# Test-time-trained attention with a SwiGLU FFN on one core: projection, x1 and FFN moved six slots forward against the scan, with z re-laid step by step

## The reference, cut to what matters

```
def step(W, kv):                       # 16 tokens of one head
    z = kc @ W
    grad = kc.T @ ((z - vc) * inv_n)
    return W - LR * grad, z
z = scan(step, eye, (rope(x @ Wk.T), x @ Wv.T))
x1 = norm(x + (norm(z) * gamma + beta) @ Wo.T)
out = norm(x1 + (silu(x1 @ gate.T * gs) * (x1 @ up.T * us)) @ down.T * ds)
```

## Time and profile before

| | us |
|---|---|
| median of 3 runs (2057.78 to 2060.44) | 2058.8 |
| the profiled execution's own time | 2054.83 |
| its span, first to last instruction | 2052.7 |
| TensorE busy | 1949.6 |
| VectorE busy | 1219.4 |
| ScalarE busy | 938.1 |
| GpSimd busy | 582.4 |

### The profile page before, as it was taken

The page is one execution under the profiler, slowest core; times in us unless marked ns, Lnnn a source line. Parts: engine busy times, 40 slices in busy tenths (PEclk is TensorE's granted clock), DMA queues, the critical chain, the costliest instruction groups (busy, mean ns, idle before and its releaser), DMA issues.

```text
span 2052.7 us, 54706 instructions
## 1 busy us (share of the span) xinstructions
PE 1949.6 (95%) x22424; PEld 1550.6 (76%) x22424; DVE 1219.4 (59%) x2814; ACT 938.1 (46%) x2258; POOL 582.4 (28%) x651
## 2 busy tenths in 40 slices
PE   5669999999999999999999999999999999998887
PEld 3347877778787777878777787877778787777775
DVE  3484665666566566656656665665666566565532
ACT  2324444444444444445444444544444454444421
POOL 2012323223332322333232233323323332332332
PEclk9769999999999999999999999999999999999999
DMA  6842222222332222232222223222222322222110
GB/s 208 265 132 82 86 88 60 82 73 86 94 88 86 61 82 71 87 95 85 89 60 83 67 90 94 87 87 59 85 73 84 94 88 86 63 82 56 49 35 21
DMA packets 211019, 176.61 MB, mean 86 GB/s; under 512 B 34193, under 2 KB 165521, under 8 KB 210577
## 3 DMA queue, kind: packets, MB, share of 16 engines
q1 hardware_dynamic: 210768, 173.08, 28.2%
HBM read 105.86 MB, written 75.76 MB: 88 GB/s over the span
## 4 chain that ended last, share of the span: by engine, by line
PE 90%; DVE 5%; ACT 2%; issue 1%; SPq 1%; DMA 1%; POOL 0%; POOLq 0%; DVEq 0%
PE gu_acc L616 35%; PE work L597 28%; PE down_acc L628 14%; PE state_acc L587 5%; PE z_acc L570 4%; PE work L604 3%; PE gu_acc L604 1%; DVE err L799 1%; DVE fm L828 1%; ACT fm L475 1%; SPq L286 1%; DVE low_half L864 1%; DVE hid L806 1%; ACT hid L451 1%; DMA v_rows<-v_scr 0%
## 5 line engine op out<-in xcount | busy, mean ns | idle before, releaser
L799 DVE TENSOR_TENSOR err<-z_acc,v_rows 32x256 f32<-32x256 f32 x1024 | 430.0, 420 | 177.8 <-PE z_acc L570 148.9
L378 POOL TENSOR_TENSOR hid_lo<-hid,hid_hi 128x256 fp32r<-128x256 f32 x352 | 267.2, 759 | 912.0 <-ACT hid_hi L461 911.9
L427 ACT ACTIVATE state<-state_acc 32x256 f32<-32x256 f32 x1028 | 385.5, 375 | 87.9 <-PE state_acc L587 63.9
L616 PE MATMUL gu_acc<-x_hi,gw 128*128 128x256 f32 x1408 | 385.8, 307 | 8.6 <-DVE x_lo L843 3.6
L616 PE MATMUL gu_acc<-x_hi,uw 128*128 128x256 f32 x1408 | 349.7, 281 | 0.0
L616 PE MATMUL gu_acc<-x_lo,gw 128*128 128x256 f32 x1408 | 349.6, 281 | 0.0
L616 PE MATMUL gu_acc<-x_lo,uw 128*128 128x256 f32 x1408 | 349.3, 281 | 0.0
L806 DVE SCALAR_TENSOR_TENSOR hid<-gu_acc,up_scale,hid 128x256 f32<-128x256 f32 x352 | 170.2, 484 | 297.3 <-ACT hid L451 296.4
L440 ACT ACTIVATE v_rows<-z_acc 128x256 f32<-128x256 f32 x256 | 98.6, 385 | 521.3 <-DVE err L799 521.3
L616 PEld LDWEIGHTS gu_acc<-x_hi,gw 128*128 128x128 f32 x1408 | 266.0, 189 | 59.8 <-DVE hid L806 23.8
L628 PE MATMUL down_acc<-dw,hid_hi 128*128 128x512 f32 x704 | 284.2, 404 | 2.8 <-POOL hid_lo L378 2.8
(11 more groups left out here) (67 smaller groups left out, 2117.3 us busy)
## 6 DMA issues: line engine op xcount, KB each, us to landing
x_fm<-xT SPq DMA_DIRECT2D x64, 256.0 KB, 3.3
k_scr<-k_tok SPq DMA_DIRECT2D x32, 512.0 KB, 2.9
k_rows<-k_scr SPq DMA_DIRECT2D x512, 32.0 KB, 1.9
v_rows<-v_scr SPq DMA_DIRECT2D x512, 32.0 KB, 1.8
z_scr<-v_rows SPq DMA_DIRECT2D x512, 32.0 KB, 1.7
z_tok<-z_scr SPq DMA_DIRECT2D x32, 512.0 KB, 3.9
x_tok<-x SPq DMA_DIRECT2D x32, 512.0 KB, 3.5
out<-x_tok SPq DMA_DIRECT2D x32, 512.0 KB, 2.9
```

The source lines that it names most:

```text
L378: pool.tensor_tensor(hid_lo[m % RING][:], hid[m % 2][:], hid_hi[m % RING][:].bitcast(F32), ALU.subtract).then_inc(hid_lo_ready, 1)
L427: act.activation(state[q, :, e].rearrange("p (r g) e -> p r g e", r=2), state_acc[q, :, 0:P].rearrange("p r (g e) -> p r g e", e=HEAD), AC ...
L616: mm = pe.matmul(gu_acc[:, k * TOK:(k + 1) * TOK], lhsT=w[:, c, m * P:(m + 1) * P].bitcast(dt), rhs=part[:, c].bitcast(dt), start=(c == 0 ...
L799: dve.tensor_tensor(err[q, g:g + 2, :, :].rearrange("p a (r h) e -> p a r (h e)", r=2), z_acc[q, :, 0:P].rearrange("p r (a c) -> p a r c", ...
```

## The change

The pipeline is cut again. Tile t is now projected within tick t (K of sequence 0 in slot 6, V in 7, K of sequence 1 in 8, V in 9 to 11, the turns of K in 12 and 13) and scanned in tick t+1. The tile scanned in the tick before has its z turned in slots 2 and 3, is projected by Wo in 4 and 5, and its x1 is turned in 8 and 9. Its FFN follows at once: `gate_up` 0 to 5 in slots 10 to 15 of the same tick (`EARLY_GU`), 6 to 10 in slots 0, 1, 2, 3 and 6 of the next (`LATE_GU`); the `down` blocks follow a slot behind, and the last layer norm is in slots 11 to 14. The ticks go from 0 to 34, 35 instead of 37.

z is stored in a layout of its own, [step, partition, 2, 128], in three transfers (steps 0 to 3, 4 to 6, 7), with both halves of each partition's row, and loaded with two 32 KB transfers per step. `k_scr` and `v_scr` are one tile deep; v's first half is loaded per sequence.

In the first two ticks: the split of V's weights comes in slot 5 of tick 0, ahead of the high part of x's second sequence on ScalarE; ScalarE issues the copies and the loads of the FFN's weights; the bias matmuls are in slot 14 of tick 0 and the split of Wo in its slot 15, ahead of the first `copy_state`; the twelve maxima are spread by `WEIGHED` over slot 3 of tick 1 to slot 5 of tick 2, and TensorE branches ahead of slot 10 of tick 2. The wait on `zeroed` before each scan half is gone. The counts are written with plain integers; `nk`, `nb`, `ncc`, `nd`, `ny` become `t`, `sc`, `o`, `f1` and `f2`, `y`.

The core of the diff (the new order of the ticks; the old one stands in the listing above):

```diff
-GU_SLOTS = (0, 1, 2, 3, 4, 5, 6, 7, 8, 11, 13)
-DOWN_SLOTS = (1, 2, 3, 4, 5, 6, 7, 8, 9, 13)
+FFN_SLOT = 10
+EARLY_GU, LATE_GU = {10: 0, 11: 1, 12: 2, 13: 3, 14: 4, 15: 5}, {0: 6, 1: 7, 2: 8, 3: 9, 6: 10}
+EARLY_DOWN, LATE_DOWN = {11: 0, 12: 1, 13: 2, 14: 3, 15: 4}, {0: 5, 1: 6, 2: 7, 4: 8, 7: 9, 9: 10}
+WEIGHED = {3: (0,), 5: (1,), 7: (2,), 9: (3,), 11: (4, 5), 13: (6, 7), 15: (8,), 17: (9,), 19: (10,), 21: (11,)}
...
-        k_scr = nc.dram_tensor("k_scr", [2, BATCH, P, DM], F32, kind="Internal").ap()
-        v_scr = nc.dram_tensor("v_scr", [2, BATCH, P, DM], F32, kind="Internal").ap()
-        z_scr = nc.dram_tensor("z_scr", [BATCH, SEQ, DM], F32, kind="Internal").ap()
+        k_scr = nc.dram_tensor("k_scr", [BATCH, P, DM], F32, kind="Internal").ap()
+        v_scr = nc.dram_tensor("v_scr", [BATCH, P, DM], F32, kind="Internal").ap()
+        z_scr = nc.dram_tensor("z_scr", [NS, P, 2, P], F32, kind="Internal").ap()
...
+            def store_z(n, i0, i1, stored):
+                if i0 == 0 and n >= 1:
+                    sp.wait_ge(zn_turned, 2 * n)
+                sp.wait_ge(z_saved, NS * n + i1)
+                sp.dma_start(z_scr[i0:i1].rearrange("i p q c -> p i q c"), v_rows[:, i0:i1]).then_inc(z_stored, 16)
+            def load_z(n, i0, i1, stored):
+                sp.wait_ge(z_stored, 48 * n + stored)
+                for i in range(i0, i1):
+                    for p in range(2):
+                        src = z_scr[i].rearrange("(h p t) q c -> p q t h c", p=2, t=MB)[p, p]
+                        dst = z_tok[i * MB:(i + 1) * MB].rearrange("t b (a p c) -> t (b a) p c", a=2, p=2)[:, :, p]
+                        sp.dma_start(dst, src).then_inc(z_tok_in, 16)
...
+                sc, o, y = t - 1, t - 2, t - 3
+                if within(sc) and sc >= 1:
+                    load_half1(sc)
+                if within(sc):
+                    store_z(sc, 0, NS // 2, 16)
+                    load_z(sc, 0, NS // 2, 16)
+                if within(t) and within(t + 1):
+                    load_x_fm(t + 1)
+                if within(t):
+                    store_v(t, 0)
+                    store_k(t)
+                    if t == 0:
+                        sp.wait_ge(state_begun, 2 * HQ)
+                    load_k_half0(t)
+                    store_v(t, 1)
+                if within(sc):
+                    store_z(sc, NS // 2, NS - 1, 32)
+                if within(t):
+                    load_v_half0(t, 0)
+                    load_v_half0(t, 1)
+                if within(sc):
+                    load_z(sc, NS // 2, NS - 1, 32)
+                    store_z(sc, NS - 1, NS, 48)
+                    load_z(sc, NS - 1, NS, 48)
+                if t == 0:
+                    load_half1(0)
+                if within(y):
+                    sp.wait_ge(y_ready, 2 * y + 2)
+                    sp.dma_start(out[:, rows(y), :].rearrange("b t f -> t b f"), y_tok[:]).then_inc(out_stored, 16)
+                if within(sc):
+                    load_x(sc)
...
+                    if within(t) and s == 6:
+                        high_x(t, 1)
+                    if within(t) and s == 8:
+                        copy_v(t, 0)
+                    if within(t) and s == 12:
+                        copy_v(t, 1)
+                    if within(o) and s == 8:
+                        high_x1(o, 0)
...
+                    if within(f2) and s in (2, 6):
+                        gate(f2, LATE_GU[s])
+                    if within(o) and s == 2:
+                        high_zn(o, 0)
+                    if within(sc):
                         if s % 2 == 0:
+                            save_z(sc, s // 2)
                         else:
+                            keep_state(sc, s // 2)
+                    if within(o) and s == 3:
+                        high_zn(o, 1)
...
+                    if t == 0 and s == 5:
                         act.wait_ge(wv_in, 16 * NC)
                         for c in range(NC):
                             high_part(wv, (x_tok, z_tok), c)
+                        for i in range(3):
+                            copy_ffn(i)
...
+                    if t == 0 and s == 15:
+                        for c in range(NC):
+                            act.wait_ge(wo_scaled, c + 1)
+                            high_part(wo, x1_tok, c)
+                        act.wait_ge(zeroed, 6)
+                        act.wait_ge(state_begun, 2 * HQ)
+                        copy_state()
+                        act.wait_ge(small_in, 16 * 7)
+                        load_ffn(0)
+                    if t == 1 and s in (3, 9):
+                        load_ffn((s + 3) // 6)
...
+            def tick(t, ffn_dt=None, first=0, last=SLOTS):
+                sc, o, f1, f2 = t - 1, t - 2, t - 2, t - 3
+                for s in range(first, last):
+                    if within(sc):
                         if s % 2 == 0:
+                            scan_z(sc, s // 2)
                         else:
+                            scan_state(sc, s // 2)
+                    if within(o) and s == 3:
+                        turn_z(o, 1)
+                    if within(o) and s in (8, 9):
+                        turn_x1(o, s - 8)
+                    if within(t) and s == 13:
                         turn_k(t, 1)
+                    if within(f2) and s in (7, 9):
+                        down(f2, LATE_DOWN[s], ffn_dt)
+                    if within(f2) and s in LATE_GU:
+                        gate_up(f2, LATE_GU[s], ffn_dt)
+                    if within(f1) and s in EARLY_GU:
+                        gate_up(f1, EARLY_GU[s], ffn_dt)
+                    if within(o) and s == 2:
+                        turn_z(o, 0)
+                    if within(o) and s in (4, 5):
+                        project_o(o, s - 4)
+                    if within(t) and s in (6, 8):
+                        project_k(t, (s - 6) // 2)
+                    if within(t) and s == 7:
+                        project_v(t, 0, 0, NC)
+                    if t == 0 and s == 9:
+                        begin_state()
+                    if within(t) and s in (9, 10, 11):
+                        project_v(t, 1, *((0, 2), (2, 3), (3, 4))[s - 9])
+                    if within(t) and s == 12:
                         turn_k(t, 0)
+                    if within(f2) and s in (0, 1, 2, 4):
+                        down(f2, LATE_DOWN[s], ffn_dt)
+                    if within(f1) and s in EARLY_DOWN:
+                        down(f1, EARLY_DOWN[s], ffn_dt)
+                    if t == 0 and s == 14:
+                        find_bias()
+            def rest(ffn_dt):
+                tick(2, ffn_dt, FFN_SLOT, SLOTS)
+                for t in range(3, NT + 3):
+                    tick(t, ffn_dt)
+            tick(0)
+            tick(1)
+            tick(2, None, 0, FFN_SLOT)
...
+                sc, o, f1, f2, y = t - 1, t - 2, t - 2, t - 3, t - 3
                 for s in range(SLOTS):
+                    if within(o) and s == 6:
+                        add_o(o, 1)
+                    if within(sc) and s % 2 == 0:
+                        scan_err(sc, s // 2)
+                    if within(o) and s == 3:
+                        low_zn(o, 1)
+                    if within(t) and s == 6:
+                        low_x(t, 1)
+                    if within(t) and s in (7, 9):
+                        rotate(t, (s - 7) // 2)
+                    if within(o) and s == 6:
+                        dve.wait_ge(o_added, 2 * o + 2)
+                        moments_of(1, o, x_tok)
+                    if within(t) and s == 13:
+                        copy_k_cols(t, 1)
+                    if within(y) and s == 11:
+                        scale_y(y)
+                    if within(y) and s == 13:
+                        dve.wait_ge(y_added, 2 * y + 2)
+                        moments_of(2, y, y_tok)
+                    if within(f2) and s in LATE_GU and s != 6:
+                        scale_hid(f2, LATE_GU[s])
+                    if within(f2) and s == 7:
+                        scale_hid(f2, 10)
+                    if within(f1) and s in EARLY_GU:
+                        scale_hid(f1, EARLY_GU[s])
+                    if within(o) and s == 0:
+                        dve.wait_ge(z_tok_in, 256 * (o + 1))
+                        moments_of(0, o, z_tok)
+                    if within(o) and s == 1:
+                        normalize(0, o, z_tok, z_tok, zn_ready)
+                    if within(o) and s == 2:
+                        low_zn(o, 0)
...
+                    if within(o) and s == 7:
+                        if o >= 2:
+                            dve.wait_ge(y_added, 2 * (o - 1))
+                            dve.wait_ge(x1_turned, 2 * (o - 1))
+                        normalize(1, o, x1_tok[o % 2], x_tok, x1_ready)
+                    if within(o) and s in (8, 9):
+                        low_x1(o, s - 8)
+                    if within(t) and s == 12:
```

(12 more changed lines are left out.)

683 lines of the change are left out of this document (266 added, 417 removed).

## The result

The changed kernel takes 2064.8 us (median of 8 runs, 2062.1 to 2067.3) where the kernel before takes 2058.8 (8 runs beside them, 2056.9 to 2060.4): a ratio of 1.0029, with a 95% interval of 1.0018 to 1.0040. It is slower by 6 us. The forecast was 2058, no change that can be measured.

A forecast was written before the change was run, and what follows sets the result against it. TensorE's own work, about 59.65 us a tick, was taken to bound the middle. Steady ticks +19, tick 31 +3, end -26 and start +3 gave -1 against the 2052.7 span; predicted median 2058 us, range 2038 to 2080.

The forecast's parts named there:

- the start's +3: Everything up to tick 3: tick 3 starts at 164 us instead of 161.1, +3 (-4 to +10).
- tick 1's 54: Tick 1: 41 for eight steps, 7 for projections, 2 to 4 for gate weights, 3 for weighings; tick 2 starts at 99.
- The first rival: Steady tick's waits stay hidden and the ends give; tick 3 starts at 158, whole 2042 us; chance 0.27.
- (a): Steady tick, first rotation, before V: only a scan half and one down cover 1.45 us; cost 0.2 us (0 to 0.4).
- (c): Steady tick, second turn of K: the copy of the first half's columns now stands behind scale_hid; cost 0.2 us (0 to 0.48).
- (d): Steady tick, first output projection: high part of z's second half comes behind the state copies; cost 0.15 us (0 to 0.4).
- (e): Steady tick, gate-up 0 to gate-up 1: 3.15 us of work between them against a 3.24 us loop; cost 0.1 us.
- (b): Steady tick, VectorE must be free when K ends: 5.0 us of queue against 5.45; margin about 0.36 us, cost 0.
- The close-up of the last gate-ups: At the end, last tile: gate-ups 9 and 10, before spaced by slots with waits, run closer; 2 us less.
- VectorE late to the first rotation: Rival, slot 7: VectorE 1 us late makes the tick pay 0.6 more, 17 us on top, 2075 us; chance 0.24.
- Waits hidden: Rival, steady tick: (a) to (e) cost 0.3 us together, +9 over the middle; whole 2042 us; chance 0.27.
- Late z: Rival, each tick: z's store and loads take 9 us instead of 5.2, moments_of waits about 1; some 2080 us; chance 0.06.

The follow-up runs named there:

- the run without cover: Changed kernel with down 9 of slot 7 moved behind the V projections, so nothing lies between scan and V: 2092.1 us, mean tick 61.29.
- the spread run: Changed kernel with only the gate copy in tick 0, gate load and two copies at 40 us, other loads after scan 1's first rows: 2057.7 us, ratio 0.9998.
- all three runs of the dose: Changed kernel with one, two or three FFN weight copies in tick 0 and the gate load behind scan 0's rows: 2059.4, 2052.0 and 2055.5 us.

## Why the prediction was wrong

**The step that failed** is the start's +3, and in it two terms. "Rows of scan 0 must share with the 8.6 MB of weight copies ... now the copies have ScalarE's queue. I take 45": the scan, whose start needs no rows of v, began at 40.98, before the 43 to 48 laid out; its first state half, which needs them, came at 65.3. The forecast had no term for the time between the two. And "2 to 4 for VectorE waiting for the gate weights" was the only price put on the loads. That 45 and tick 1's 54 should have given 99 for tick 2; it was 111.9. The working had the evidence in hand, the v store of 23.4 us behind the same copies, and set it aside because the copies had another queue. The runs showed that the queue gave no protection: the store took 24.2 us behind three copies on ScalarE's queue too. In the kernel before that delay fell where hardly anyone waited (VectorE 1.60 us), behind the last loads of scan 0's first rows in the same queue (the copies began at 37.7) and with scan 1's rows not needed until 98.8. The change moved K and V to the middle of the tick. From their stores to the scan that needs them there is now less than half a tick, and the z transfers stand in the same queue. Without the traffic tick 3 starts at 157, 7 us before the 164 laid out. The work itself was priced too long, and this hid a part of the miss. The first rival's 158 is near that number, but it was meant with the traffic.

**The steady tick** held in its terms: (a) 0.20 of 0.2, (c) 0.20 of 0.2, (d) 0.14 of 0.15, (e) 0.13 of 0.1, and the turn of z at 0.20 as before. The mean of ticks 4 to 30 grew from 59.84 to 60.35, by 0.51 and not by 0.67; the dropped waits on `zeroed` did not give the 0.16. Cut at the first matmul of each block and averaged over ticks 4 to 29, the scan halves of a tick grew by 0.44 us, the downs by 0.07 and the projections by 0.06, while the gate-ups fell by 0.05 and the turns by 0.01. With the four waits taken off, every kind of block is 0.01 to 0.05 shorter, and that is the 0.16: the kernel before had small waits beyond the 0.19 that the forecast took for the only one, and "In the middle a new order can only add waits" was not quite true. (b) was right at 0, though its rows leave a margin of 0.45 and not 0.36: V waits for the rotation itself and no longer than (a) has it. The +16.5 is 27 times 0.51, tick 31's 3.8 (forecast as 3) and 0.9 less in tick 3.

**The end** was forecast at -26 and came at -24.9. The close-up of the last gate-ups, -2, didn't come.

**Rivals.** VectorE late to the first rotation: no, though the run without cover shows its price, 27 us for 0.94 a tick. Waits hidden: no, all four show. Late z: not in the steady state, where the turn of z waits 0.20 as it did; the Trainium skill's rule on small transfers (DMA: Bandwidth & Descriptors, Rules for kernel authors) has no trace there. In tick 2 of the spread run it was z that paid, 15.45 us, but to weight loads and not to its own small pieces.

The same page of the Trainium skill, in its section on queues, rings and completion order, says that a DMA engine goes round its queues packet by packet and finishes a packet before it turns to the next. Two queues would then share one set of engines, which the forecast did not weigh when it took ScalarE's queue for a protection. The trace agrees with the sharing: 24.2 us behind three copies from another queue. It does not look like taking turns, by which one would expect 256 KB to be through long before 8.6 MB: the store landed about 2 us after the last copy in all three runs of the dose, as if it stood in line behind them. How much of that is the held issue of the last section, no run here shows.

## What to carry to other kernels

A transfer of megabytes is not free merely because its own result is needed late: price it by the small transfers of every queue that will be issued while it moves, and ask who waits for those. When work moves later relative to its consumer, check what bulk traffic its old slack was hiding, here in the first three ticks and not in the steady state; and when a wait goes from place to place with each new layout, run both kernels without the suspected traffic, which gives the two floors at once.

## What was not expected of the hardware

An issue on SyncE took 8.6 us with two copies under way on ScalarE's queue and 18.7 with three, against 0.34 with one: the issuing engine itself is held. So all that stands behind it in its program is late as well. It is not the number of copies alone: in the kernel before, with three copies ahead in SyncE's own queue, the store at 44.15 was issued in 0.35 us and still landed 23.4 us later, and it was the loads of v's rows at 57.33 that were held (9.65 us for eight). What decides how long an issue is held, no run shows.

The kernel before varies by a few us from execution to execution, and its profiled one was 4 us below its median. In the run of the old order without weights, the last 16.5 us of tick 31 have a mean granted clock of 0.74, a part of them at the lower of the levels 1.2 and 2.4 GHz, and TensorE busy for 11.4; tick 31 lasted 59.5 us. In the profiled execution of before, the same stretch:

```profile
1880.00:1894.70 14.70, 9.44 (x166) 7.12 (x165) 8.33 (x20) 7.93 (x21) 2.15 (x3) 1.00 0.04 8
```

Full clock, and the tick took 56.7. These 3 us would fit most of the distance between that profile and the median, and with it most of why the medians differ by 6.0 where the two profiles differ by 11; the changed kernel's tick 31 is full and has no such stretch. No further profile was taken, but the mean granted clocks of the other executions point the same way: of those of the kernel before that ran beside the experiments, the twelve at 0.976 to 0.978 took 2055.8 us on average and the 55 at 0.973 or 0.974 2058.4, and the profiled one had 0.977. Where in the kernel their clock was lower is not shown. Nor does the stretch explain the other nine runs of the order without weights, 2059.4 to 2063.7 us: the profiled one, with the stretch, took 2057.0.
